# Where the stores of the decay factors are begun: SyncE's queue at the border of the batches, or ScalarE's in the middle of one

## The reference

```python
dt = softplus(dt_raw + dt_bias); dA = dt * A            # [batch, tokens, heads]
dA_cum = cumsum(dA within a chunk)
Y_diag  = einsum(C, B, exp(dA_cum[t] - dA_cum[s]), x * dt)      # inside a chunk
chunk_decay = exp(dA_cum[:, :, -1, :])                          # one factor a chunk and head
state = state * chunk_decay + states                            # from chunk to chunk
Y_off   = einsum(C, state_before, exp(dA_cum))                  # what earlier chunks give
```

## Time and profile before

| | |
|---|---|
| runs of the kernel | 2007.36, 2013.19, 2015.89 us, median 2013.19 |
| the profiled execution | 2006.9 us, of which the span from the first to the last instruction is 2005.1 |
| busy over the span | PE 87%, DVE 71%, POOL 50%, ACT 46% |
| body of one batch | 163.3 to 166.8 us (7 of them up to 1220 us), then the last one, then 630 us of feed-forward |
| issues of the stores in question | 32 of `e_dram<-ecs` (32 KB, 1.5 us from issue to landing), 32 of `end_dram<-ends` (0.5 KB, 1.3 us) |

### The profile page before, as it was taken

The page is one execution under the profiler, slowest core; times in us unless marked ns, Lnnn a source line. Parts: engine busy times, 40 slices in busy tenths (PEclk is TensorE's granted clock), DMA queues, the critical chain, the costliest instruction groups (busy, mean ns, idle before and its releaser), DMA issues. The chain is left out here.

```text
span 2005.1 us, 37560 instructions
## 1 busy us (share of the span) xinstructions
PE 1736.9 (87%) x11168; PEld 872.1 (43%) x11168; DVE 1419.8 (71%) x2295; ACT 920.8 (46%) x1647; POOL 995.4 (50%) x1031
## 2 busy tenths in 40 slices
PE   3688889898888888888979888788999999999998
PEld 1245445444544544454544544444434334334333
DVE  6768668857857766876785776885676776766765
ACT  2453253353434335325334433434574564664753
POOL 0045436515525543543552653675674674764754
PEclk9897898898888888888889888888999999999999
DMA  6110140131123014113113202822011011010110
GB/s 203 47 47 24 40 95 26 42 68 50 37 46 88 24 40 101 31 35 79 35 42 64 66 24 52 214 49 57 17 48 63 11 52 39 29 58 26 37 43 32
DMA packets 214648, 109.35 MB, mean 55 GB/s; under 512 B 133796, under 2 KB 185696, under 8 KB 214496
## 3 DMA queue, kind: packets, MB, share of 16 engines
q1 hardware_dynamic: 214496, 107.37, 20.1%
HBM read 80.57 MB, written 26.76 MB: 54 GB/s over the span
## 5 line engine op out<-in xcount | busy, mean ns | idle before, releaser
L1024 ACT ACTIVATE decay<-ps_d 128x512 f32<-128x512 f32 x256 | 151.6, 593 | 332.5 <-PE ps_d L771 270.1
L713 PE MATMUL ps_in<-u_hi,w_hi 128*128 128x512 f16 (+1 forms) x608 | 237.3, 390 | 57.3 <-DVE u_lo L1197 35.6
L1299 DVE TENSOR_TENSOR mix<-decay,gb 128x512 f32<-128x512 f32 x256 | 224.3, 881 | 61.9 <-PE ps_yd L783 26.7
L1610 POOL TENSOR_TENSOR xend<-xpad,decay 128x256 f32<-128x256 f32 x256 | 178.7, 718 | 163.4 <-PE ps_yo L806 131.6
L735 PE MATMUL ps_in<-w_out,zg 128*128 128x512 f32 x512 | 254.3, 654 | 6.1 <-DVE pre L1210 6.1
L713 PE MATMUL ps_in<-u_lo,w_hi 128*128 128x512 f16 (+1 forms) x608 | 236.4, 389 | 0.0
L713 PE MATMUL ps_in<-u_hi,w_lo 128*128 128x512 f16 (+1 forms) x608 | 236.0, 388 | 0.0
L1210 DVE SCALAR_TENSOR_TENSOR pre<-ps_in,cws,pre 128x511 f32<-128x511 f32 (+2 forms) x240 | 178.9, 746 | 8.6 <-ACT pre L963 2.8
L793 PE MATMUL ps_yo<-bc,state 128*128 128x64 f32 x896 | 152.2, 341 | 17.2 <-DVE state L1314 17.2
L735 PEld LDWEIGHTS ps_in<-w_out,zg 128*128 128x128 f32 x512 | 108.0, 218 | 134.2 <-issue 125.4
L963 ACT ACTIVATE pre<-ps_in,cb,cws 128x512 f32<-128x512 f32 x80 | 62.2, 778 | 208.9 <-PE ps_in L713 208.8
(11 more groups left out here) (194 smaller groups left out, 3932.3 us busy)
## 6 DMA issues: line engine op xcount, KB each, us to landing
ebc<-e_dram SPq DMA_DIRECT2D x256, 64.0 KB, 2.6
u<-u_t SPq DMA_DIRECT2D x9, 1024.0 KB, 5.4
res<-u_tok SPq DMA_DIRECT2D x32, 256.0 KB, 2.7
x_dram<-res SPq DMA_DIRECT2D x32, 256.0 KB, 2.0
xa<-x_dram SPq DMA_DIRECT2D x8, 1024.0 KB, 5.5
xr<-x_dram SPq DMA_DIRECT2D x32, 256.0 KB, 2.7
out<-xr SPq DMA_DIRECT2D x32, 256.0 KB, 2.0
fw_words<-gu_words SPq DMA_DIRECT2D x32, 176.0 KB, 2.9
```

Of the source, the lines that this page charges most:

```text
L713: last = mm(ps_in[bk][0:m, :], w[:, k, col:col + m], u[:, k, :], start=(k == 0 and j == 0), stop=(k == KT - 1 and j == 2))
L1024: ac(decay[:, n % NG, :, :].rearrange("p a b -> p (a b)"), ps_d[n % 2][:, :], ACT.Exp).then_inc(e_done, 1)
L1299: v.tensor_tensor(mix[:, n % NG, :, :], decay[:, n % NG, :, :], gb[:, c % 2, 0:CH].unsqueeze(1).broadcast_to([P, CT, CH]), ALU.mult).then_ ...
L1610: g_.tensor_tensor(xend[:, pairs, :], xpad[:, c % 2, pairs, :], decay[:, g, :, CH - 1:CH].broadcast_to([P, CT, 2 * HD]), ALU.mult).then_in ...
```

## The change

The function `store_factors` moves from SyncE's program to ScalarE's and is cut in two: one call stores one half of the tokens with 4 transfers. In the bodies of batches 0 to 6 ScalarE calls it at the end of slot 22 and of slot 24, and in the prologue it calls both, one behind the other, after the first tap of x5. SyncE's `load_head` ends with the rows of chunk 1. The transfers themselves, their sizes and their semaphore are as before.

```diff
--- before.py
+++ after.py
@@ -454,21 +454,6 @@
                             sp.dma_start(ld_dram[b, :, :, j, h2, t].rearrange("r e t -> e r t"), ld_parts[heads, :, :])\
                               .then_inc(parts_out, 16)
 
-            def store_factors(b):
-
-                sp.wait_ge(ecs_done, b + 1)
-                settled(sp)
-                sp.wait_ge(ends_done, b + 1)
-                settled(sp)
-                for token_half in range(2):
-                    t, row = slice(token_half * LH, (token_half + 1) * LH), token_half * NH
-                    chunks = slice(token_half * NC // 2, (token_half + 1) * NC // 2)
-                    for h2 in range(2):
-                        rows = slice(row + h2 * NP, row + (h2 + 1) * NP)
-                        sp.dma_start(e_dram[b].rearrange("(q h) t -> h q t", h=2)[h2][:, t], ecs[rows, :]).then_inc(e_out, 16)
-                        sp.dma_start(end_dram[b].rearrange("(q h) c -> h q c", h=2)[h2][:, chunks], ends[rows, :])\
-                          .then_inc(e_out, 16)
-
             def load_dec(b):
 
                 sp.wait_ge(e_out, (b + 1) * E_OUT)
@@ -550,7 +535,6 @@
                 settled(sp)
                 load_rows(b, 0)
                 load_rows(b, 1)
-                store_factors(b)
 
             def room_free(last):
 
@@ -950,6 +934,20 @@
                 ac(ecs[:, :], dte[:, :], ACT.Exp).then_inc(ecs_done, 1)
                 ac(ends[:, :], dte[:, CH - 1:LH:CH], ACT.Exp).then_inc(ends_done, 1)
 
+            def store_factors(b, token_half):
+
+                act.wait_ge(ecs_done, b + 1)
+                settled(act)
+                act.wait_ge(ends_done, b + 1)
+                settled(act)
+                t, row = slice(token_half * LH, (token_half + 1) * LH), token_half * NH
+                chunks = slice(token_half * NC // 2, (token_half + 1) * NC // 2)
+                for h2 in range(2):
+                    rows = slice(row + h2 * NP, row + (h2 + 1) * NP)
+                    act.dma_start(e_dram[b].rearrange("(q h) t -> h q t", h=2)[h2][:, t], ecs[rows, :]).then_inc(e_out, 16)
+                    act.dma_start(end_dram[b].rearrange("(q h) c -> h q c", h=2)[h2][:, chunks], ends[rows, :])\
+                       .then_inc(e_out, 16)
+
             def ln_dt(b):
                 act.wait_ge(dt_dve, b * DT_STEPS + 15)
                 ac(dtc[:, :], dta[:, :], ACT.Ln).then_inc(dt_act, 1)
@@ -1041,6 +1039,8 @@
                     if st.proj is not None and n == 20:
                         exp_cs(st.proj)
                         ln_dt(st.proj)
+                    if st.proj is not None and n in (22, 24):
+                        store_factors(st.proj, (22, 24).index(n))
                 tail(st)
 
             def turn(f, tiles):
@@ -1100,6 +1100,9 @@
                     ln_dt(0)
                 if i == 4:
                     exp_cs(0)
+                if i == 5:
+                    for token_half in range(2):
+                        store_factors(0, token_half)
                 if i in (3, 5):
                     weights_hi(i // 2 + 2)
             act.wait_ge(const_in, N_CONST)
```

## The result

The changed kernel takes 2024.8 us (median of 7 runs, 2021.54 to 2028.87), the kernel before on the same chip 2005.92 (7 runs, 2000.43 to 2015.89). The ratio is 1.0092, with a 95% interval of 1.0066 to 1.0118: the change makes the kernel about 19 us slower. The forecast was 2010.7 with a range up to 2019.0. The profiled span is 2027.1 us, 22.0 us over the 2005.1 of before; the mean granted clock is 0.916 against 0.919.

What follows compares the result with a forecast made beforehand. The prediction took TensorE and its waits as the bound. Borders 0, slots 0 and prologue +0.4 gave 2007.3 us on the fastest execution (2006.9); from the middle of four, 2010.3, it forecast 2010.7, range 2003.4 to about 2019.

Steps and rivals of the forecast that it cites:

- The sum: Whole kernel: 0 at seven borders, 0 in fourteen slots, +0.4 us in the prologue, 2007.3 us against the profiled execution.
- dear issues: Rival, slower: an issue costs ScalarE 1.63 us, delaying prologue and slot 24, together 2026.8 us; 8 in 100.
- Border, gain 0: SyncE at 7 borders: removing 4.0 us of issues only lengthens its wait for VectorE before the x store; gain 0.
- Slots 22 and 24, cost 0: ScalarE in the bodies: four issues of 0.50 us per slot fit, group 28 starts 0.9 us late; cost 0.
- Prologue, +0.4: ScalarE in the prologue: eight issues, 4.0 us, delay the last weight block's rounding and make `bc` 0.4 us late.
- The queueing of two engines: Rival: ScalarE stands back while SyncE issues in the prologue, term at most 5.2 us, up to 2012.1; 15 in 100.
- An earlier SyncE: Rival, faster: 4.0 us freed at borders covers TensorE's waits for `lhs_d`, at most 23.4 us, 1983.5; 4 in 100.
- The clock: Rival: a moved pause changes which batch gets which granted clock, bodies 3.5 us apart; 13 in 100.

Runs made afterwards that it cites:

- e3: Changed kernel with 40 do-nothing semaphore increments padded ahead of SyncE's loop and 60 ahead of ScalarE's: 2007.42 us, ratio 1.0004.
- e6: Kernel before with the hardware loop over batches 1 to 6 written out on all five engines: 2007.06 us, ratio 1.0009.
- e7: Changed kernel with the hardware loop over batches 1 to 6 written out on all five engines: 2006.57 us, ratio 1.0001.
- e1: Changed kernel with 40 semaphore increments padded ahead of SyncE's loop only: 2013.8 us, ratio 1.0029.
- e5: Kernel before, no transfer moved, with 25 semaphore increments padded ahead of ScalarE's loop only: 2011.73 us, ratio 1.0031.
- e4: Kernel before, no transfer moved, with 30 semaphore increments padded ahead of SyncE's loop and 50 ahead of ScalarE's: 2018.57 us, ratio 1.0054.
- e2: Changed kernel with 60 semaphore increments padded ahead of ScalarE's loop only: 2023.13 us, ratio 1.0071.
- e10: Kernel before with its loop written out and 32 semaphore increments on ScalarE at the head of bodies 1 to 6: 2006.89 us, ratio 1.0006.
- e8: Changed kernel with 90 semaphore increments padded ahead of SyncE's loop and 60 ahead of ScalarE's: 2018.26 us in one run.
- e12: Kernel before, no transfer moved, with 18 semaphore increments padded ahead of SyncE's loop only: 2018.55 us in one run.
- e11: Kernel before with its loop written out and 48 semaphore increments on ScalarE at the head of bodies 1 to 6: 2017.03 us, ratio 1.0061.

## Why the prediction was wrong

**The failed step is "The sum": 0 at seven borders, 0 in fourteen slots, +0.4 in the prologue.** It had no term for what the change does to the programs as such. The 26 instructions fewer in SyncE's loop and the 28 more in ScalarE's were costed by their durations only, and so were the instructions that left and joined the prologue ahead of the loops. At each of the five turns both engines then stop for a fetch of their own instructions, and the five windows behind the turns are 20.6 us longer. None of the four rivals held this mechanism; the answer on the slower side (dear issues) came near in size, 2026.8, for a reason that did not occur.

**Border, gain 0: right.** SyncE's x store waits behind the rows of chunk 1 for 914.06 - 906.33 = 7.7 us, forecast about 7.5. e3, e6 and e7 show nothing gained from the earlier stores.

**Slots 22 and 24, cost 0: right.** The price was taken as 0.50 us a step and is 0.49. Group 28 is 0.35 us later than before relative to its neighbours, forecast 0.9. The issues need less of ScalarE than I had allowed, since some begin beside an activation.

**Prologue, +0.4: too dear by 0.4, measured 0.0.** The timeline of ScalarE after:

```profile
71.50 0.78 ACT L961 ACTIVATE pre<-ps_in,cb,cws 128x512 f32<-128x512 f32 x1 [1.64 <-PE ps_in L697]
71.69 0.41 ACTq L947 DMA_DIRECT2D e_dram<-ecs  x1
...
75.03 0.44 ACTq L948 DMA_DIRECT2D end_dram<-ends  x1
75.52 2.56 ACT L1079 ACTIVATE w_hi<-zg,scal 128x512 f16<-128x512 f32 x4 [3.24 <-issue]
78.00 0.78 ACT L961 ACTIVATE pre<-ps_in,cb,cws 128x512 f32<-128x512 f32 x1
...
83.84 1.06 ACT L972 ACTIVATE bc<-pre 128x1024 f32<-128x1024 f32 x1 [1.08 <-DVE pre L1213]
```
and the first tap of x5 before:

```profile
72.16 0.78 ACT L963 ACTIVATE pre<-ps_in,cb,cws 128x512 f32<-128x512 f32 x1 [1.65 <-PE ps_in L713]
```

This profiled execution is 0.66 us ahead already at that tap, before the first moved store, so times have to be taken from it. The eight issues take 3.8 us and begin during the tap. The rounding starts 4.02 us behind the tap's start and was 0.68 behind it, 3.3 us later and not 4.0, since the issues begin beside the tap. That fits into the 3.27 us of idle time behind it: the tap of x6 starts 6.50 us behind that of x5 in both kernels. `bc` starts 12.34 us behind it and was 12.33: the term is 0.0 where 0.4 was forecast.

**The queueing of two engines (rival): not seen.** While ScalarE issues from 71.69 on, SyncE's eight `ld_dram` (70.74 to 73.67) take 2.93 us, and took 2.92. Seven of ScalarE's eight issues are 0.41 to 0.45 us long, against 0.32 in the loop, together 0.83 us. The Trainium skill, Perfetto Trace Analysis, section DMA Instruction — HWDGE (DVE, Sync), has the wait for the descriptor maker's lock inside such an issue. These rows do not show it: the issues at 74.08 and 74.56 are 0.44 and 0.45 us long while SyncE issues nothing, and so is this one in the body of batch 0, where SyncE is silent from 190 to 216 us:

```profile
198.45 0.44 ACTq L947 DMA_DIRECT2D e_dram<-ecs  x1
```

**Dear issues (rival): refuted**, 0.32 us against the 1.63 assumed. **An earlier SyncE (rival): did not occur**; the waits for `lhs_d` rose to 31.6 us from the 23.4 of the earlier trace rows, and without the stops they are 23.0 (e3). **The clock (rival):** not the cause, since TensorE is busy for 4.4 us less in the five windows; it takes part as an answer to the pauses.

**What the 22 us are made of.** SyncE's stop delays the loads at the head of a body and with them the rows of chunk 2; ScalarE's delays slot 0. Alone, ScalarE's costs 0.3% (e1, e5), SyncE's 0.5 to 0.7% (e4, e2), both 0.9%. That is less than stops times turns, 5 x (4.5 + 2.6) = 35 us. By the five windows TensorE stands only 25.0 us longer, so some 10 us of the stops do not reach it, and 4.4 us of the 25.0 come back in its busy time, as in e10. This is an account of one profiled execution each, and no run separates the terms.

**What stays open.** Which rule decides where a loop turns freely. The Trainium skill, Runtime: NRT & Kernel Launch, section Instruction fetch mechanics, says that most engines hold only two blocks of their program, refill them one after the other, and that a taken branch to a target outside stops the engine until the block is fetched. Rows and runs here agree with the stop. They do not show its block of 16 KiB, 256 instructions, for these engines: the packets of queue 14 are 8.2 KB, and those of queue 8 16.4 KB (1.46 MB / 89). Nor do two blocks of 256 give SyncE's six entries of the table, wherever they are laid. From its figures (16 KiB, 256 instructions, so 64 bytes each) I estimate 128 instructions in a packet of queue 14. With three such blocks held, a loop turns freely when it touches no more than three, and that one rule, with a fixed count of instructions ahead of each program that the trace does not record (43 to 51 on SyncE, 65 to 77 on ScalarE), gives every entry of the table, 11 different placements. Once e1 to e4 had narrowed the counts it foresaw e5 and e8, and it left e12 open; by it the kernel before had 9 to 17 instructions of room on SyncE. It is a fit, not a measurement, and four blocks of 96 fit the table as well. Why SyncE's stop is 5.1 to 5.5 us with its head at 204 and 3.2 to 3.9 us elsewhere, I have only argued: by the same fit the head then stands in the last few instructions of a block, so a second fetch follows at once.

## What to carry to other kernels

A hardware loop can have a price at its turn that depends on where its program stands: here loops of 294 to 356 instructions turned freely in one place and stopped in another, and 18 instructions made the difference. So when an edit adds or removes instructions inside or ahead of such a loop, count them per engine, compare the packets of the instruction queues before and after, and look at the gap at each turn, before the time is put down to what the edit was about. If the packets have jumped, pad the prologue and measure again: only then do two versions stand on the same ground. And where TensorE answers a pause with a higher granted clock, as here, do not expect a removed pause of 1.5 us to show in the time.

## What was not expected of the hardware

- An engine's stop for its own instructions at a turn is 2.3 to 4.0 us on ScalarE and 3.2 to 5.5 us on SyncE (0.75 of it stands there in the kernel before too), and the profile names another engine, or "issue", for it.
- Issues of transfers on ScalarE run beside its own activations: an issue of 0.34 us at 867.73 is followed by one at 868.23, while `sq` runs from 868.13 to 868.76.
- Writing the loop out did not make the kernel faster (e6, 1.0009), and its bodies are as long as the good ones of before. The Trainium skill, Runtime: NRT & Kernel Launch, section Instruction fetch mechanics, says that kernels prefer full unrolling where possible; in these runs it takes every stop away and the time stays.
- A pause of 1.57 us in each of six bodies cost nothing, one of 2.64 us 0.6% of the whole (e11 against the kernel before).
